# DLRM tower on one core: field pairs in three groups of 8, 8 and 10 in place of two of 13, and a new order of TensorE's work between tile 0 and tile 1

## What is computed

```python
    return jnp.einsum('bik,bjk,hij->bhk', x_prev, x0, W) + b[None, :, None]
...
x1 = _cin_layer(inputs, inputs, W1, b1)
x2 = _cin_layer(x1, inputs, W2, b2)
res = jnp.concatenate([x1, x2], axis=1)
return jnp.sum(res, axis=-1)
...
h = jnp.concatenate([z, dense_ctx], axis=1)
h = jnp.maximum(h @ W_top1 + b_top1, 0.0)
h = jnp.maximum(h @ W_top2 + b_top2, 0.0)
y = h @ W_top3
```

## Time and profile before

| | |
|---|---|
| median of 3 runs | 164.32 us (164.03 to 164.59) |
| the profiled execution: its own time / its span | 164.4 us / 162.7 us |
| busy in that span: TensorE matmuls | 152.3 us (94%), 1261 records |
| VectorE | 110.6 us (68%) |
| ScalarE | 84.4 us (52%) |
| GpSimd | 70.4 us (43%) |
| mean granted TensorE clock | 0.989 of full |

### The profile page before, as it was taken

The page is one execution under the profiler, slowest core; times in us unless marked ns, Lnnn a source line. Parts: engine busy times, 40 slices in busy tenths (PEclk is TensorE's granted clock), DMA queues, the critical chain, the costliest instruction groups (busy, mean ns, idle before and its releaser), DMA issues.

```text
span 162.7 us, 3320 instructions
## 1 busy us (share of the span) xinstructions
PE 152.3 (94%) x1261; PEld 143.7 (88%) x1261; DVE 110.6 (68%) x342; ACT 84.4 (52%) x225; POOL 70.4 (43%) x76
## 2 busy tenths in 40 slices
PE   6989999699925999999999999999999999999994
PEld 6979899599914999998999999999999899999993
DVE  5829899999999495996667799455788952241000
ACT  1133479689660639654444676344448644560032
POOL 2777777726478272466455366437360000000000
PEclk9999999999996999999999999999999999999999
DMA  4998011055700022000010101001010000000000
GB/s 150 357 400 310 16 14 16 12 175 158 265 4 8 10 65 96 12 12 12 5 19 6 12 8 16 8 10 18 5 16 0 4 0 0 4 0 0 0 4 1
DMA packets 4930, 9.07 MB, mean 56 GB/s; under 512 B 1617, under 2 KB 3217, under 8 KB 4914
## 3 DMA queue, kind: packets, MB, share of 16 engines
q1 hardware_dynamic: 2130, 6.25, 11.0%
q0 software_dynamic: 2176, 1.12, 4.8%
q10 hardware_dynamic: 608, 1.49, 2.5%
HBM read 8.85 MB, written 0.00 MB: 54 GB/s over the span
## 4 chain that ended last, share of the span: by engine, by line
PE 61%; DVE 16%; POOL 10%; issue 4%; ACT 4%; DMA 4%; DVEq 0%; ACTq 0%
PE bank L367 13%; PE bank L380 13%; POOL rows L284 10%; DVE folded L741 9%; PE bank L375 8%; PE bank L314 8%; PE bank L419 5%; PE bank L389 4%; DVE prod L900 2%; ACT diag L557 2%; DMA idx<-in_ids_dram 2%; PE bank L409 2%; PE bank L407 2%; PE bank L412 2%; PE bank L396 2%
## 5 line engine op out<-in xcount | busy, mean ns | idle before, releaser
L284 POOL DMA_INDIRECT rows<-in_tbl_dram,idx x68 | 69.5, 1022 | 50.0 <-DMA rows<-in_tbl_dram,idx 30.6
L367 PE MATMUL bank<-diag,prod 128*128 128x108 f32 x256 | 31.4, 276 | 1.6 <-DVE prod L900 1.6
L367 PEld LDWEIGHTS bank<-diag,prod 128*128 128x128 f32 x256 | 30.3, 192 | 2.3 <-issue 2.0
L314 PE MATMUL bank<-small,idb 128*128 128x256 f32 (+1 forms) x72 | 22.6, 423 | 5.1 <-DVE w1p L680 4.6
L733 DVE COPY t<-bank 13x128 f32<-13x128 f32 (+2 forms) x48 | 12.6, 263 | 20.8 <-PE bank L375 20.3
L380 PEld LDWEIGHTS bank<-t,v 128*128 128x128 f32 x208 | 24.6, 192 | 1.4
L530 ACT COPY t<-bank 128x432 f32<-128x432 f32 x32 | 15.0, 522 | 19.4 <-PE bank L367 19.3
L380 PE MATMUL bank<-t,v 128*128 128x128 f32 x208 | 25.0, 276 | 0.0
L557 ACT ACTIVATE diag<-prod,quad 128x416 f32<-128x416 f32 (+2 forms) x44 | 20.9, 554 | 5.5 <-DVE prod L696 5.5
L680 DVE TENSOR_TENSOR w1p<-bank,chosen 128x320 f32<-128x320 f32 (+2 forms) x28 | 15.0, 536 | 9.1 <-PE bank L314 7.8
L375 PE MATMUL bank<-diag,prod 128*77 128x64 f32 x256 | 20.1, 230 | 0.0
(11 more groups left out here) (71 smaller groups left out, 172.6 us busy)
## 6 DMA issues: line engine op xcount, KB each, us to landing
idb<-in_idt_dram SPq DMA_DIRECT2D x4, 576.0 KB, 5.8
rows<-in_tbl_dram,idx POOLq DMA_INDIRECT x68, 2.4
wt<-in_W_top_dram SPq DMA_DIRECT2D x2, 512.0 KB
w2t<-in_w2t_dram SPq DMA_DIRECT2D x1, 768.0 KB, 12.0
small<-in_small_dram SPq DMA_DIRECT2D x1, 672.0 KB, 9.1
w1t<-in_w1t_dram SPq DMA_DIRECT2D x1, 640.0 KB, 4.1
small<-in_small_dram SPq DMA_DIRECT2D x1, 608.0 KB, 10.6
w1p<-in_w1p_dram ACTq DMA_DIRECT2D x1, 521.0 KB, 3.9
```

The lines of the kernel that those rows point to most:

```text
L284: pool.indirect_dma_start(rows[t][:, f, :], None, tables[f], bass.IndirectOffsetOnAxis(ap=idx[:, t, f:f + 1], axis=0)).then_inc(s_got[t][p ...
L314: mm = nc.tensor.matmul(ps[:, c], onehot[:, t % 2, e * P:(e + 1) * P], small[:, SPLACE[e]:SPLACE[e + 1]], start=True, stop=True)
L367: mm = nc.tensor.matmul(m0[:, g % GBANK, :, 0:JW], prod[:, G, 0:P], diag[:, G, :, :], start=True, stop=True)
```

## The change

The 26 fields are reordered and cut into groups B (8 fields), C (8) and A (10). Kept pairs are those inside each group, 36 + 36 + 55, a column of ones, and the 64 products of a field of B and a field of C: 192 columns, 64 of them beyond the first 128.

- The weight sets: `fold` for the first 16 fields has only the first 128 columns, four fields to a PSUM bank; for the last 10 fields it has 192. `ctB` is 16 matmuls of 224 columns and `ctA` 10 of 160, in place of 26 of 169. VectorE's additions are `last_terms` (17 instructions, 2560 elements for each partition) and `low_terms` (34, 2624), in place of 95 instructions with 4999.
- The high pairs are needed for 10 fields only, and there are exactly 64 of them: `v1` has 5 slots of full 128 rows in place of 8 with the last of 55, so `z2_low` is 5 matmuls. `z1` is 1 + 3 in place of 1 + 4. The second matmul of a group in a step has 80 stationary and 4 x 11 = 44 moving columns in place of 77 and 64.
- The parts are 16, 7 and 3 fields in place of 13, 10 and 3; the small tables' fields are 7 of the first part and 2 of the second (5 and 4 before). `products_low` has 9 instructions for 136 pair columns, `products_last` 16 instructions (two for each 4 groups) for 55.
- w1p grows from 1042 to 1280 columns (640 KB). `W2PARTS` become fields 0 to 3 and 4 to 15 on ScalarE's queue (256 and 768 KB) and 16 to 25 on SyncE's (640 KB). The first look-up comes behind the second set instead of the third.
- TensorE's transposes of `v0` (last 10 fields) and `v1` and ten matmuls of z2 come ahead of tile 1's third look-up; the other look-ups are spread behind them.

```diff
-HALF = FIELDS // 2
-SHIFTS = HALF // 2 + 1
+NB, NA = 8, 10
+A0 = 2 * NB
+SHIFTS = NA // 2
...
-C, D = (0, 5), (5, 6)
-JLOW = 11
...
+PB = [sum(2 * (NB - e) for e in range(d)) for d in range(NB + 1)]
+PA = PB[NB]
+PHALF = PA + SHIFTS * NA
+PONE = PHALF + NA // 2
+PBC = PONE + 1
+PAIRS = PBC + NB * NB
+assert PONE == P - 1 and A0 + NA == FIELDS
...
-COL_A = P + 64
-COL_B = COL_A + HALF
-PCOLS = COL_B + HALF + WRAP
-M1 = 64 + HALF
-CROSS = HALF * HALF
...
+COL_B = PAIRS
+COL_A = COL_B + A0
+PCOLS = COL_A + NA + WRAP
+M1 = PAIRS - P + A0
...
+CROSS_A = A0 * NA
+CROSS_B = NB * NB + 2 * NA * NB
...
-GRAM = J1 // 2
-GSLOTS = 4
+GRAM = NA // 2
+GSLOTS = 3
...
-PARTS = [(0, 13, COL_A, 5), (13, 23, COL_B, 17), (23, 26, COL_B + 10, 23)]
+PARTS = [(0, A0, COL_B, 7), (A0, 23, COL_A, 18), (23, FIELDS, COL_A + 23 - A0, 23)]
-PACE = [0, 0, 0, 0, 0, 1, 2, 3, 3, 4, 5, 6, 7, 8, 9, 10, 12, 13, 14, 15, 17, 18]
+PACE = [0, 0, 0, 0, 0, 1, 1, 2, 3, 4, 5, 6, 7, 8, 10, 11, 13, 14, 16, 17, 18, 19]
-PAUSES = [(0, 7), (0, 10), (1, 17), (1, 21), (2, 25)]
+PAUSES = [(0, 9), (0, 12), (0, 15), (1, 21), (2, 25)]
-SMALL = [0, 1, 2, 3, 4, 13, 14, 15, 16]
+SMALL = [0, 1, 2, 3, 4, 5, 6, 16, 17]
-NEEDS = [3, 7, 7]
+NEEDS = [5, 7, 7]
-W2PARTS = [(0, 6), (6, 14), (14, 26)]
+W2PARTS = [(0, 4), (4, 16), (16, 26)]
...
-SETUP = [("fold", j, 2) for j in range(0, FIELDS, 2)]
-SETUP += [("ctA", x, min(3, HALF - x)) for x in range(0, HALF, 3)]
-SETUP += [("ctB", x, min(3, HALF - x)) for x in range(0, HALF, 3)]
-SETUP += [("v0", j, min(4, FIELDS - j)) for j in range(HALF, FIELDS, 4)]
-SETUP += [("v1", x, min(4, J1 - 1 - x)) for x in range(0, J1 - 1, 4)]
-SETUP += [("v0", j, min(4, HALF - j)) for j in range(0, HALF, 4)]
+SETUP = [("fold", j, 4) for j in range(0, A0, 4)] + [("fold", j, 2) for j in range(A0, FIELDS, 2)]
+SETUP += [("ctB", x, 2) for x in range(0, A0, 2)]
+SETUP += [("ctA", x, min(3, NA - x)) for x in range(0, NA, 3)]
+SETUP += [("v0", j, min(4, FIELDS - j)) for j in range(A0, FIELDS, 4)]
+SETUP += [("v1", x, min(4, NA - x)) for x in range(0, NA, 4)]
+SETUP += [("v0", j, 4) for j in range(0, A0, 4)]
...
-BEHIND = {2: 0, 3: 1, 4: 2, 5: 3, 6: 4, 7: 5, 8: 6}
+BEHIND = {1: 0, 2: 1, 3: 2, 4: 3, 5: 4, 6: 5, 7: 6}
...
             def z2_low(t, end):
                 pe.wait_ge(s_e1, (t + 1) * STEPS)
                 for x in range(GRAM):
-                    k = slice(0, C1 if x == GRAM - 1 else 64 + C1)
-                    mm = nc.tensor.matmul(Z2[:, 0:P], v1[k, x, :], t1[k, x, :], start=False, stop=end and x == GRAM - 1)
+                    mm = nc.tensor.matmul(Z2[:, 0:P], v1[:, x, :], t1[:, x, :], start=False, stop=end and x == GRAM - 1)
...
             pe.wait_ge(s_eg, STEPS - 1)
-            for q in range(DONE["ctB"], HIGH):
-                if HOME[q] == 3:
-                    pe.wait_ge(s_e0, STEPS)
+            for q in range(CROSSES, HIGH):
                 make(q)
-            look_up(1, 2)
+            pe.wait_ge(s_e0, STEPS)
             for q in range(HIGH, DONE["v1"]):
                 make(q)
+            pe.wait_ge(s_sf, HIGH)
+            z2(0, NA)
+            look_up(1, 2)
             look_up(1, 3)
-            pe.wait_ge(s_sf, HIGH)
-            z2(0, 7)
-            look_up(1, 4)
-            look_up(1, 5)
-            z2(7, HALF)
-            look_up(1, 6)
-            pe.wait_ge(s_eg, STEPS)
             for q in range(DONE["v1"], len(SETUP)):
                 make(q)
             pe.wait_ge(s_sf, DONE["v1"])
             z2_low(0, False)
+            look_up(1, 4)
+            look_up(1, 5)
             pe.wait_ge(s_sf, len(SETUP))
-            z2(HALF, FIELDS, True)
+            z2(NA, 18)
+            look_up(1, 6)
+            z2(18, FIELDS, True)
+            pe.wait_ge(s_eg, STEPS)
             pe.wait_ge(s_pad, 1)
...
             one_hot(1)
+            dve.wait_ge(s_sf, DONE["ctB"])
+            terms = last_terms(fold_a, ct_b)
+            add(terms, 0, False)
+            add(terms, 1, True)
             dve.wait_ge(s_sf, DONE["ctA"])
-            low = low_terms(folded)
-            add(low, 0, False)
-            add(low, 1, True)
-            cross = cross_a(folded, ct[0])
-            add(cross, 0, False)
-            add(cross, 1, True)
-            dve.wait_ge(s_sf, DONE["ctB"])
-            cross = cross_b(folded, ct[1])
-            add(cross, 0, False)
-            add(cross, 1, True)
+            terms = low_terms(fold_b, ct_a, ct_b)
+            add(terms, 0, False)
+            add(terms, 1, True)
...
+def products_low(eng, prod, factor):
+
+    for d in range(NB):
+        n = NB - d
+        eng.tensor_tensor(prod[:, :, PB[d]:PB[d + 1]].rearrange("p g (c i) -> p g c i", c=2),
+                          with_dims(factor[:, :, 0:], (A0, GROUPS), (NB, 2), (1, n)),
+                          with_dims(prod[:, 0, COL_B + d:], (PCOLS, GROUPS), (NB, 2), (1, n)), ALU.mult)
+    return eng.tensor_tensor(prod[:, :, PBC:PAIRS].rearrange("p g (b c) -> p g b c", c=NB),
+                             with_dims(factor[:, :, 0:], (A0, GROUPS), (1, NB), (0, NB)),
+                             with_dims(prod[:, 0, COL_B + NB:], (PCOLS, GROUPS), (0, NB), (1, NB)), ALU.mult)
+
+
+def products_last(eng, prod, factor, g0, groups):
+
+    g = slice(g0, g0 + groups)
+    eng.tensor_tensor(prod[:, g, PA:PHALF].rearrange("p g (d i) -> p g d i", i=NA),
+                      with_dims(factor[:, g, :], (NA, groups), (0, SHIFTS), (1, NA)),
+                      with_dims(prod[:, g, COL_A:], (PCOLS, groups), (1, SHIFTS), (1, NA)), ALU.mult)
+    return eng.tensor_tensor(prod[:, g, PHALF:PONE], factor[:, g, 0:NA // 2],
+                             prod[:, g, COL_A + SHIFTS:COL_A + 2 * SHIFTS], ALU.mult)
```

More of the change, by code:

```diff
@@ L428, in layer3 @@
                 mm.then_inc(s_l3, 1)
-            for q in range(DONE["ctB"]):
+            for q in range(CROSSES):
                 make(q)
@@ L895, in products_b @@
[L895 to L917 removed]
+    side = NB * CROSS_B + X_AC - X_AB - (X_AB - X_CB)
@@ L932, in layouts @@
     cols = pair_columns()
[L933 removed]
+    w1p = np.zeros((P, 2, WCOLS), np.float32)
     for c, pair in enumerate(cols):
```

289 lines of the change are left out of this document (124 added, 165 removed).

## The result

The change is slower: 167.58 us median of 4 runs (165.83 to 170.11) against 164.25 (164.03 to 164.59) beside it, a ratio of 1.015 [1.008, 1.023]. Timed twice more on other chips it gave 1.010 [1.003, 1.018] and 1.012 [1.008, 1.017]. The forecast, 162.2 us within 160.2 to 164.6 and faster with 0.75, was wrong in its sign and its range. A ratio here leaves out the runs over 1.5 per cent above a version's shortest (one of the change's four, 170.11); since such runs have the low clocks that are at issue, the ratio of the medians of all runs, here 1.020, is given beside it where the two read differently.

What follows compares the result with a forecast made beforehand. TensorE alone was taken to bound the kernel from 72.16 us on, changing hands before. Tile 1 -0.85, middle tiles -0.1 and last tile -1.1 sum to -2.05, giving 162.2 us, range 160.2 to 164.6.

Steps and rivals of the forecast that it cites:

- I take 12.0: Start-up: w2t's second piece, needed by TensorE's second fold at 9.3, lands at 12.0 us, between 11.2 and 12.7.
- All 51 in 12.2 us: Tile 0 to tile 1: VectorE's 51 weight additions take 12.2 us, from about 37.0 to 49.2, covered by TensorE's new order.
- Layer 2 will wait about 0.8: Tiles 0 to 2: TensorE waits some 0.8 us each for a ReLU ahead of layer 2.
- Middle tiles -0.1 for two: Middle tiles: -0.05 us each, as TensorE's gain turns into a wait for VectorE's longer products.
- Last tile -1.1: Last tile: nothing follows, so TensorE's -1.29 us and the steps' +0.16 give -1.1 us.
- dearer products: Rival: VectorE's products cost more than the fit; at 0.6 us more each, 164.6 us in all; chance 0.08.
- moving columns: Rival: moving columns bind the small pair matmuls, 1.07 us a tile, giving 160.1 us; chance 0.03.
- a reorder that doesn't work: Rival: additions run as long as before, to 52.3, and the look-up behind z2 waits: about +1.8, 164.0 us; chance 0.07.
- middle tiles that follow TensorE: Rival: products or spread are quicker than worked out, -1.05 us twice more, 160.2 us; chance 0.08.
- the start-up sum of +2.1: Start-up: w2t at 12.0, fold group 0.89, 1.24 to first pick; last pick of tile 0 at 21.7 against 19.56.
- the rival's 165.1: Rival: TensorE's clock falls in the start-up gap, w2t landing at 13.2, 1.7 us of matmul time lost; slower; chance 0.12.
- Tile 0 to tile 1: From first Gram matmul at 32.9 to tile 1 at 71.3 us against 72.16: -0.85, the 4.65 us idle gone.

Runs made afterwards that it cites:

- w2t-only version: Kernel before with only W2PARTS changed, to the change's (0,4), (4,16), (16,26): 1.011 [1.007, 1.014] of the kernel before.
- the third transpose alone: The change with the third transpose of tiles 1 to 3 ahead of the first part's products on VectorE: 0.984 [0.980, 0.988] of the kernel before.
- the filling alone: The change with four unread matmuls ahead of layer 2 in tiles 0 to 2: 1.005 [1.002, 1.009] of the kernel before; median of all runs 166.68 us.
- the second chip: The change itself, unaltered, timed again on another chip where every kernel spread more: 1.010 [1.003, 1.018] of the kernel before; medians of all runs 1.030.
- the version with both fillings: The change with eleven unread matmuls in the start-up gap and four ahead of layer 2 in tiles 0 to 2: 0.996 [0.993, 0.998], 164.25 us.

## Why the prediction was wrong, point by point

- **"I take 12.0" for w2t**: right, 11.96. **"All 51 in 12.2 us"**: 12.8 (38.85 to 51.61). **Products 5.11**: 5.16 (26.41 to 31.57). **z2_low 1.11**: 1.12 to the next row (97.27 to 98.39). **The 80-column matmuls at 141 ns**: eight in 1.11, 139 ns. **Layer 2 will wait about 0.8**: 0.94 and 1.01. **Middle tiles -0.1 for two**: +0.14. **Last tile -1.1**: -1.2. The rivals of dearer products, of moving columns, of a reorder that doesn't work and of middle tiles that follow TensorE all fell.
- **The step that failed: the start-up sum of +2.1 at the last pick**, which took the fold group behind the wait for w2t at full speed (0.89 us), with "a granted clock of 1.00 behind it". ("The idle 4.65 us are gone and the clock stays up" held where it was said, ahead of the look-ups, but not behind the new wait ahead of z1.) The prediction named the mechanism as a rival and priced it out: "2.7 us is nearer the short ones", so it should decide only "from w2t at about 12.9". At 11.96, behind a gap of only 2.03 us, the clock fell all the same. (By the mean clocks of the w2t-only version it fell there in eight runs of twelve, which is inferred.) The picks came 1.8 us later than the sum, the first Gram matmul 2.15. Three gaps of one run were too few to bound the lowest one that does harm. That the rival's 165.1 lies near the shortest runs (165.8) is an accident: it was worked out for w2t at 13.2, with one place of loss where there are several.
- **The step that was missing.** "Tile 0 to tile 1" followed TensorE, VectorE and ScalarE and never costed GpSimd, though `PACE` and `PAUSES` stood in the diff. Gathers paced by the folds start late with them, and then meet VectorE's additions: one gather's instruction took 4.00 us where most take 0.94. Before, the additions met gathers too, but none took over 2.44, and the second transpose didn't wait. Here it waited 2.58 us. Of the 3.55 us at tile 1, 2.15 were there at the first Gram matmul, and the first transpose of tile 1 came 2.2 late (60.15 against 57.95); the other 1.4 lie between it and the products, where this wait stands. In runs with the low clock behind the first Gram matmul the picks are as late as the rows, and the wait doesn't show (64.79 with the third transpose alone): there the two losses cover each other.
- **The middle tiles.** That TensorE's 1.13 us turn into a wait was right, and moving the third transpose showed it. Whether the wait costs more than its own length is not shown in general: the filling alone took 0.15 per cent off the median. On the second chip, where the waits were 1.94 and 2.25 us, layer 2 behind them took 2.72 and 3.50 us where it has 2.05 at the full clock.
- **The sum, redone.** Late landing +1.3 (w2t-only version); falls of the clock, with what follows from them, +2.7 (from 166.93 to 164.25, the change to the version with both fillings, of different chips whose kernels before differ by 0.5, so rather 2.2). Measured is +2.0 in all, so the rest of the change is worth -1.5 to -2. That last term is what is left over and has no run of its own, and the landing was priced in the kernel before: the sum is an estimate and proves nothing.

## What to carry to other kernels

A landing that moves behind the first work of an engine costs its own lateness, then the clock behind the gap, then whatever is paced by that engine's output: cost all three, and cost every queue whose pacing numbers the diff touches. Where an engine's gain turns into a wait, move the producer's last step (here one short transpose) ahead of the work that grew, before counting the gain as lost. And fill a wait with work nobody reads as a test: where the filling ends before the wait does, it tells the price of the clock from the price of the wait. Take enough runs for it, and look at all of them: the versions here differ in how many runs have the low clock, and a ratio of the shorter runs alone showed a gain of 0.7 per cent that the median of all doesn't have.
